# Cross attention kernel: the first three maxima of a group move from its neighbour's first tiles to the last two tiles of the group before that

## What is computed

```python
c_attn_w = jax.nn.softmax(jnp.einsum('bhqd,bhsd->bhqs', q_c, k_c) * scale, axis=-1)
c_attn_out = jnp.einsum('bhqs,bhsd->bhqd', c_attn_w, v_c)
```

## Time and profile before

| | us |
|---|---|
| median of three runs | 6480.61 |
| lowest, highest | 6472.38, 6483.08 |
| the profiled execution | 6475.3 |
| its span | 6473.5 |

### The profile page before, as it was taken

One profiled execution on the slowest core, in us unless ns is written; L12 is line 12 of the kernel. 1 busy time (PEld: TensorE's weight loads), 2 busy tenths in 40 slices (PEclk: granted clock), 3 DMA queues, 4 the chain that ended last, 5 costly groups with the idle time before them and its releaser, 6 DMA issues.

```text
span 6473.5 us, 147216 instructions
## 1 busy us (share of the span) xinstructions
PE 5939.3 (92%) x49714; PEld 3112.4 (48%) x49714; DVE 4119.5 (64%) x6523; ACT 4237.2 (65%) x8158; POOL 981.5 (15%) x1660
## 2 busy tenths in 40 slices
PE   6999999999877899999999977789999999999998
PEld 3444444444444444544454444444444444445665
DVE  5767677677555667766776445467777777754443
ACT  3777777777666577777777556557777777773333
POOL 3121121121111111111111011212212212200000
PEclk9999999999999899999999989899999999999999
DMA  2322322222111322232232011122232232220110
GB/s 88 78 65 56 79 59 63 75 56 69 42 57 61 82 68 65 69 79 69 57 76 75 1 57 57 55 77 68 57 77 68 57 77 68 57 65 21 54 53 29
DMA packets 180915, 402.05 MB, mean 62 GB/s; under 512 B 16992, under 2 KB 124560, under 8 KB 166416
## 3 DMA queue, kind: packets, MB, share of 16 engines
q1 hardware_dynamic: 180752, 400.01, 22.9%
HBM read 316.81 MB, written 83.14 MB: 62 GB/s over the span
## 4 chain that ended last, share of the span: by engine, by line
PE 73%; issue 8%; ACT 8%; DVE 7%; DMA 2%; SPq 1%; POOL 1%; ACTq 0%; DVEq 0%; POOLq 0%
PE bank L1140 19%; PE bank L1186 18%; PE pair L1156 14%; DVE MX L1480 3%; PE bank L1112 2%; ACT P L1316 2%; PE bank L1107 2%; DMA QP<-scr_q 2%; PE pair L1173 2%; PE pair L1162 1%; PE bank L699 1%; PE bank L690 1%; ACT QP L1327 1%; PE pair L626 1%; DVE ST L1437 1%
## 5 line engine op out<-in xcount | busy, mean ns | idle before, releaser
L1316 ACT ACTIVATE P<-bank 128x512 f32<-128x512 f32 (+1 forms) x5504 | 3102.2, 597 | 1350.6 <-PE bank L1140 1306.9
L1480 DVE TENSOR_REDUCE MX<-pair 128x2 f32<-128x802 f32 x3072 | 2923.9, 988 | 1296.3 <-PE pair L1156 1288.0
L1140 PE MATMUL bank<-QP,KP 128*128 128x256 bf16 (+1 forms) x11008 | 2091.3, 277 | 141.7 <-ACT P L1316 90.0
L1186 PE MATMUL bank<-P,VA 128*25 128x256 f32 (+1 forms) x22016 | 1756.0, 391 | 5.8 <-issue 0.5
L1156 PE MATMUL pair<-KP,QP 96*128 96x401 bf16 x6144 | 1576.0, 338 | 60.9 <-DMA QP<-scr_q 42.3
L1140 PEld LDWEIGHTS bank<-QP,KP 128*128 128x128 bf16 (+1 forms) x11008 | 858.0, 100 | 1577.3 <-ACT P L1316 912.9
L1186 PEld LDWEIGHTS bank<-P,VA 128*25 128x25 f32 (+1 forms) x22016 | 401.7, 102 | 711.0 <-issue 456.7
L1156 PEld LDWEIGHTS pair<-KP,QP 96*128 96x128 bf16 x6144 | 593.5, 98 | 181.7 <-DVE MX L1480 64.0
L1605 POOL COPY VA<-VN 128x416 f32<-128x416 f32 (+1 forms) x320 | 138.6, 434 | 2520.6 <-PE bank L1186 2439.1
L1484 DVE TENSOR_REDUCE MX<-pair 128x4 f32<-128x1024 f32 x256 | 311.3, 1223 | 326.8 <-PE pair L1162 326.2
L1327 ACT CAST QP<-pair 2x512 bf16<-2x512 f32 x640 | 338.9, 575 | 130.1 <-PE pair L1173 124.7
(11 more groups left out here) (246 smaller groups left out, 4497.5 us busy)
## 6 DMA issues: line engine op xcount, KB each, us to landing
KP<-scr_k SPq DMA_DIRECT2D x192, 900.6 KB
QP<-scr_q SPq DMA_DIRECT2D x960, 48.0 KB
CN<-ctx_n SPq DMA_DIRECT2D x40, 768.0 KB
scr_k<-KSF SPq DMA_DIRECT2D x48, 600.8 KB, 3.3
scr_k<-KSF SPq DMA_DIRECT2D x48, 600.0 KB, 3.3
CT<-ctx_t SPq DMA_DIRECT2D x24, 800.5 KB, 4.4
KP<-scr_ks SPq DMA_DIRECT2D x128, 144.0 KB
scr_q<-QS SPq DMA_DIRECT2D x80, 192.0 KB, 2.1
```

Source lines behind the costliest of these rows:

```text
L1140: last = nc.tensor.matmul(SC[half][0:kt, k * N:(k + 1) * N], KP[g][:, c0:c0 + kt], QP[g][:, h * N:(h + 1) * N], start=True, stop=True)
L1186: last = nc.tensor.matmul(OB[32 * h:32 * h + STEP + HD + 1, 0:N], VA[g % 2][0:kt, t, h, :], P[(g * ph.nt + t) % 2][0:kt, h * N:(h + 1) * N ...
L1316: nc.scalar.activation(P[v % 2][0:kt, half * 2 * N:(half + 1) * 2 * N], SC[half][0:kt, :], ACT.Exp, scale=SCALE).then_inc(sem("probs_full" ...
L1480: nc.vector.tensor_reduce(MX[:, r, c:c + 2], MP[j % 2][:, :].rearrange("p (t k) -> p t k", t=2)[:, :, 0:SPANS[0][1]], AX.X, ALU.max).then_ ...
```

## The change

The maxima of a cross group start two tiles sooner (`EARLY = 2`). Steps 0, 1 (tile 11) and 2 (tile 12) of a group now stand in the last two tiles of the group *two ahead of it*, steps 3 to 15 in tiles 0 to 8 of the group ahead of it. The row products and their copies move from tile 11 to tile 10. Groups run through from one element to the next: tile 11 of group 2 now holds steps 0 and 1 of group 0 of the next element, tile 11 of group 3 those of its group 1. Where the next element is of a self phase, nothing is taken ahead. Where a cross phase starts, steps 0 to 2 of group 1 follow the maxima of group 0 in one piece. TensorE and VectorE change in the same way; the loads and pieces keep their places.

```diff
@@ -19,6 +19,7 @@
 B, N, D = 16, 256, 128
 S = 1601
 H, HD = 16, 8
+EARLY = 2
 G = 4
 NG = H // G
 NPAIR = NG // 2
@@ -133,7 +134,7 @@
             split_stored=16 + 16 * len(self.key_stores), stream_done=1 if self.gate is not None else 0,
             **{"packed_loaded%d" % g: 64 for g in range(NG)}), B)
 
-        self.shift_tile = self.nt - 2 if self.cross else self.nt - 1
+        self.shift_tile = self.nt - 3 if self.cross else self.nt - 1
 
     def after(self):
         return self.c.after()
@@ -143,6 +144,11 @@
         t, n = slot
         spread = max(n - 2, 1)
         return [j for j in range(self.nm) if min(j * spread // self.nm, n - 1) == t]
+
+    def early(self, first, end):
+
+        spread = self.nt - 2
+        return [j for j in range(self.nm) if first <= j * spread // self.nm < end]
 
     def prep_slots(self, host):
 
@@ -183,6 +189,28 @@
         self.pieces = sorted(pieces, key=lambda x: x[0])
         self.uses = [(role, n) for _, role, n in self.pieces if n not in NO_BANK]
         self.slots = 1 if ph is None else ph.nt * NG
+
+    def group(self, g):
+
+        return (self.ph, self.b, g) if g < NG else (*self.nxt, g - NG) if self.nxt else None
+
+    def maxima(self, g, t):
+
+
+        ahead, far, nt = self.group(g + 1), self.group(g + 2), self.ph.nt
+        if not self.ph.cross or not ahead or not ahead[0].cross:
+            return [(*ahead, j) for j in ahead[0].maximum_at((t, nt))] if ahead else []
+        if t >= nt - EARLY:
+            p = t - (nt - EARLY)
+            return [(*far, j) for j in far[0].early(p, p + 1)] if far and far[0].cross else []
+        return [(*ahead, j) for j in ahead[0].early(t + EARLY, t + EARLY + 1)]
+
+    def maxima_behind(self, g, t):
+
+
+        if self.ph.cross or g < NG - 1 or t < self.ph.nt - 1 or not self.nxt or not self.nxt[0].cross:
+            return []
+        return [(*self.nxt, 1, j) for j in self.nxt[0].early(0, EARLY)]
 
     def owner(self, role):
         return {"post": self.prev, "prep": self.nxt}[role]
@@ -1192,28 +1220,30 @@
                 ph, b = el.ph, el.b
                 last_tile = (el.prev[0], el.prev[1], NG - 1, el.prev[0].nt - 1) if el.prev else None
                 for g in range(NG):
-                    ahead = (ph, b, g + 1) if g + 1 < NG else (*el.nxt, 0) if el.nxt else None
+                    ahead = el.group(g + 1)
                     for t in range(ph.nt):
-                        js = ahead[0].maximum_at((t, ph.nt)) if ahead else []
+                        js = el.maxima(g, t)
                         third = -(-len(js) // 3)
                         among, behind = el.here(g * ph.nt + t)
                         scores(ph, b, g, t, 0)
                         for j in js[:third]:
-                            maximum(*ahead, j)
+                            maximum(*j)
                         for piece_ in among:
                             piece(el, *piece_)
                         scores(ph, b, g, t, 1)
                         for j in js[third:2 * third]:
-                            maximum(*ahead, j)
+                            maximum(*j)
                         if last_tile:
                             head_values(*last_tile)
                         last_tile = (ph, b, g, t)
                         for j in js[2 * third:]:
-                            maximum(*ahead, j)
+                            maximum(*j)
                         if ahead and t == ph.shift_tile:
                             shift_rows(*ahead)
                         for piece_ in behind:
                             piece(el, *piece_)
+                        for j in el.maxima_behind(g, t):
+                            maximum(*j)
 
             for ph in plan:
                 if isinstance(ph, Phase):
@@ -1225,6 +1255,9 @@
                         for j in range(ph.nm):
                             maximum(ph, 0, 0, j)
                         shift_rows(ph, 0, 0)
+                        if ph.cross:
+                            for j in ph.early(0, EARLY):
+                                maximum(ph, 0, 1, j)
                     if ph is plan[0]:
                         pe.wait_ge(sem("rest_loaded"), 32)
                         for k, a in enumerate(ATT):
@@ -1500,22 +1533,23 @@
             def element(el):
                 ph, b = el.ph, el.b
                 for g in range(NG):
-                    ahead = (ph, b, g + 1) if g + 1 < NG else (*el.nxt, 0) if el.nxt else None
                     for t in range(ph.nt):
                         among, behind = el.here(g * ph.nt + t)
-                        mine = ahead[0].maximum_at((t, ph.nt)) if ahead else []
+                        mine = el.maxima(g, t)
                         third = -(-len(mine) // 3)
                         for j in mine[:third]:
-                            maximum(*ahead, j)
+                            maximum(*j)
                         if not ph.cross:
                             for piece_ in among:
                                 piece(el, *piece_)
                         for j in mine[third:]:
-                            maximum(*ahead, j)
-                        if mine and mine[-1] == ahead[0].nm - 1:
-                            shifts(*ahead)
+                            maximum(*j)
+                        if mine and mine[-1][3] == mine[-1][0].nm - 1:
+                            shifts(*mine[-1][:3])
                         for piece_ in (among if ph.cross else []) + behind:
                             piece(el, *piece_)
+                        for j in el.maxima_behind(g, t):
+                            maximum(*j)
 
             for ph in plan:
                 if isinstance(ph, Phase):
```

## The result

Four executions of the changed kernel took 6702.19 to 6724.14 us, median 6711.88; the kernel before on the same chip 6472.38 to 6484.24, median 6481.84. The ratio is 1.0357, 95% interval 1.0336 to 1.0377: **3.6% slower**. The profiled execution took 6720.0 us, its span is 6718.2. The forecast was 6653. The direction held, the time lies in the stated range of 6560 to 6715 but only 3 us from its upper end, and the size was 59 us short: +173 forecast, +230 measured against this kernel before.

The account below looks back on a forecast made before the run. TensorE, busy 92% of the span, was taken to bound the kernel. +142 - 49 + 0 + 4 + 76 = +173 on the profiled 6475.3 us gave 6648, or 6653 us against the median, 2.7% slower; range 6560 to 6715.

Parts of the forecast that it names:

- Worse: Rival: handover wait 4 us, each low-clock stretch the full 7; 6752 us at the outer end, some 6710 mid; chance 0.11.
- (a): Handovers between elements of a cross phase: TensorE waits 3.16 us for group 0's load, 45 times, +142 us.
- (e): Behind each handover's DMA wait: TensorE's clock falls to half, costing 1.7 us a handover, +76 us.
- The rival without the clock: Handovers of cross phases: the DMA wait comes but the clock does not fall; +97, 6578 us; chance 0.24.
- (b): Change of group: TensorE's 0.54 us wait for exponentials becomes about 0.2 for row copies; 1.0 us an element, -49 us.
- (c): Group 0 of a0 and c2: the 1.1 us shift wait goes, ScalarE waits for statistics instead; costed at nothing.
- (d): Starts of the three cross phases: maxima 0 to 2 of group 1 made in one piece, +4 us.

Follow-up runs that it names:

- e4: The changed kernel with the last two key projections (k2, k3) two slots sooner, at 24 and 26: 6526.89 us, 1.0071.
- e1: The changed kernel with only the maxima of the next element's group 0 kept out of group 2, standing denser in group 3: 6535.15 us, 1.0089.
- e3: The changed kernel with 16 matmuls, results overwritten, ahead of each handover's wait on the load, 720 in all: 6647.64 us, 1.0258.
- e2: The kernel before with only maximum step 0 of the next element's group 0 moved to tile 11 of group 2: 6657.52 us, 1.0273.
- e10: The changed kernel with the logarithm at slot 13 instead of 12 and key projections k2, k3 at slots 24 and 26: 6482.76 us, 1.0002.
- e5: The kernel before with key projections k2 and k3 at slots 24 and 26 in place of 26 and 28: 6494.22 us, 1.0023.
- e11: The changed kernel with the logarithm at slot 13 and key projections k2, k3 at slots 25 and 26: 6497.65 us, 1.0030.
- e12: The kernel before with the logarithm at slot 13 and key projections k2, k3 at slots 25 and 26: 6488.13 us, 1.0014.

## Why the prediction was right, and where not

The direction was right, and so were the two main causes, the wait and the clock; the forecast of +173 was 57 us too small against the measured +230. The middle of the rival "Worse", 6710 us, is almost the measured time, but by other means: it had waits of 4 us and low stretches of 7. The waits were 3.0 us, and the clock record of c1 has 4.9 us at the low clock an element. That rival hit the number by chance.

**(a) The DMA wait, +142: right.** 179.1 - 42.3 = 137 us, 3.04 in each of 45 handovers against 3.16; e4 and e1 take it away.

**(e) The clock, +76: right in size.** e3 gives 64 and e2, at 2.5 us waits, 66. The 64 are net: in e3 the clock fell at the end of group 0 in 17 of the same 30 elements of a0 and c2, against 13 in the changed kernel. In c1, which has no such second fall, e3 gains 1.95 us an element, more than the 1.7 forecast. The rows from which the 45% was read are four score and eight value products, twelve and not eight; the ratio of 1.83 to 1.01 us stands. In the handover shown the slow rows run from 2511.62 to 2514.96, 3.3 us of work and not 3.8. The rival without the clock is out. The Trainium skill, "TensorE: Matmul & The Clock Gate", section "HAM oscillation — how this bites in real kernels", says that a loop in which each step waits for a DMA starts each step at half clock; the trace agrees in the main, with the clock at 0.57 behind the wait shown and 64 us that return once it is filled. But not each step is paid for: in c1 the clock stayed at 1.00 behind 2 of 15 waits of about 3 us, and in e2 behind 6 of 15, each of 2.4 to 2.8 us. Which waits are spared these runs do not tell.

**(b) The change of group, -49: mis-sized.** The waits moved as the prediction said: in c1 the 0.54 us on the exponentials is gone, and step 1 waits for the copies, 6.7/16 = 0.42 us in the changed kernel, against 0.2 forecast, and 4.9/17 = 0.29 in e10. These means hold only the two waits of an element that the profile shows as idle; there are four. But the copies did not start 0.42 us behind the row products. In a0 the products start at 1172.05 and the copies at 1172.65, since ScalarE is still at the exponentials of tile 10. The rest lies in TensorE's busy time. Windows over the same 14 elements of c1, the kernel before and then e10:

```profile
2210.00:3519.61 1309.61, 1281.60 (x11820) 646.26 (x11817) 914.67 (x1149) 967.76 (x1834) 187.11 (x266) 1.00 0.27 70
2216.96:3523.23 1306.27, 1291.66 (x11821) 641.79 (x11819) 921.06 (x1149) 969.30 (x1834) 186.93 (x266) 1.00 0.27 70
```

The idle time of an element fell from 28.01/14 = 2.00 to 14.61/14 = 1.04 us, by the 1.0 that was forecast. But the busy time rose by 10.06/14 = 0.72, with the same matmuls and the clock at 1.00, so that the period won 0.24. Most of the 0.72 are waits that do not show as idle. At the first change of group of an e10 element step 1 starts 0.73 us behind the first of the scores ahead of it, and 0.35 of that are idle; step 0, which waits for nothing, starts 0.23 behind its own:

```profile
2600.79 0.39 PE L1168 MATMUL bank<-QP,KP 128*128 128x256 bf16 x2
2601.02 0.51 PE L1184 MATMUL pair<-KP,QP 96*128 96x401 bf16 x2
2601.36 0.38 PE L1168 MATMUL bank<-QP,KP 128*128 128x256 bf16 x2
2602.09 0.52 PE L1184 MATMUL pair<-KP,QP 96*128 96x401 bf16 x2 [0.35 <-ACT QP L1360]
```

At the other three changes the distances are 0.42, 0.61 and 0.32. The four delays of step 1 add up to 1.2 us, and the idle times to only 0.6: what of a wait lies beneath the row ahead of it counts as busy. What the moved maxima are worth with the load in time, over the whole kernel, is e10 less e5, which has its key slots but not its logarithm's, -11 us; e11 less e12, with the same slots on both sides, +10; and e10 less the kernel before, +4. The forecast gain of 49 us is in none of them.

**(c) The shift wait, 0: the step that failed.** The prediction named the cover (VectorE is late, and ScalarE will wait for the statistics) and took ScalarE's wait as the old one in another place. It was a dearer one. In the earlier trace rows the logarithm at 1020.22 came behind work and waited for nothing; with three maxima ahead of the last statistics it waited 1.99 us, the exponentials behind it held TensorE, and in 13 of 30 elements TensorE's clock fell there too. Moving the logarithm one tile gives 48 us back (44 from e4 to e10), about half of it waits and half busy time. I had asked who is late next, and not who is queued behind the late one.

**(d)** The three starts, +4, cannot be told apart.

The terms by measurement: +137 (a), +65 (e), +48 (c), and -11 to +10 for (b) with (d), 239 to 260; the medians give 230 to 233. They need not add up exactly: (c) and (e) meet in a0 and c2, where without the falls at the handover more came at the end of group 0 (17 for 13). So the two terms that the forecast had wrong are (c), 48 us too low, and (b), with (d) 35 to 55 us too low.

## What to carry to other kernels

Before a consumer is moved ahead, compare how long its load takes from issue to use with the new distance: here 9.4 us against 6.5, and two slots sooner for the producer took back 185 of 233 us. Cost a wait of TensorE of 2.5 to 3 us by half as much again for the clock behind it (66 on 113 us in e2, 64 on 137 in the changed kernel). Do not count won idle time as won time before the busy time is compared too. When a wait changes engines, look at what stands behind the waiting instruction on the new engine: a logarithm that nobody needed soon held exponentials that TensorE needed at once.

## What was not expected

- The clock fell without any DMA wait near. In the element shown it did so behind idle times of 0.66, 0.57 and 0.37 us within 3.5 us (1176.88 to 1180.34); the window from 1180 to 1183 of the changed kernel stands at 0.54. Columns as in the earlier trace rows:

```profile
1180.00:1183.00 3.00, 2.66 (x15) 0.94 (x16) 2.17 (x3) 1.21 (x3) 3.00 (x8) 0.54 0.00 0
```

  The same three waits left it at 1.00 elsewhere (560 to 570), so they can bring it down and need not. In the kernel before, 1.10 and 0.43 us in much the same place did not: the scores behind them took 0.39 us, as at the full clock. The Trainium skill, "TensorE: Matmul & The Clock Gate", section "A second HAM failure mode: psum-queue depth-cycling", tells of short idles between groups of matmuls that make the clock swing, in a kernel that cycles through PSUM banks in each iteration; this row agrees as to the short idles, which here come from waits on two other engines.
- Filling a wait with useless matmuls made the kernel 64 us faster: 720 matmuls more, and TensorE's real work at the full clock.
- One slot of one projection in c1 is worth 1.3 us an element (e10 and e11), more than the 1.0 us that the prediction hoped to win at the changes of group.
